# Gathering the first experts' rows, norm and top-k projection: three stages or one

## What is computed

```
h = attn0(x); h = concat(cls, h)
h = h + attn1(layernorm(h))                  # causal, rotary
h = h + moe(layernorm(h))                    # 8 gated experts, top 2
h = h + topk_attn(layernorm(h), Wq, Wk, Wv)  # 16 heads, 32 largest scores kept
h = h + selu_experts(layernorm(h))            # gate picks 2 of its logits
```

## Time and profile before

| | us |
|---|---|
| median of 3 runs (lowest, highest) | 2140.19 (2139.48, 2140.79) |
| profiled execution, its own time | 2137.56 |
| its span | 2135.8 |
| PE busy in the span | 1445.6 (68%) |
| DVE busy | 1470.7 (69%) |
| ACT busy | 825.2 (39%) |
| POOL busy | 583.4 (27%) |

### The profile page before, as it was taken

How to read it: one execution, slowest core, us unless ns; L and a number is a source line. 1 busy time by engine, 2 the same in 40 slices (tenths; PEclk the granted TensorE clock), 3 DMA queues, 4 the chain that set the end, 5 groups by cost and what they waited for, 6 DMA issues and landing times. The chain is left out here.

```text
span 2135.8 us, 35245 instructions
## 1 busy us (share of the span) xinstructions
PE 1445.6 (68%) x10364; PEld 861.4 (40%) x10397; DVE 1470.7 (69%) x4775; ACT 825.2 (39%) x2043; POOL 583.4 (27%) x1036
## 2 busy tenths in 40 slices
PE   6488887958888614999809266766676666667651
PEld 3122224524444412666505144544454445445540
DVE  3578885657777620111135499989998999899955
ACT  2266664215555301222203244444444544454430
POOL 4100001210000032000063245444554455445530
PEclk9699998969999856999958657666766677666765
DMA  5572220352330511111134600110021002100001
GB/s 161 170 258 78 75 71 8 113 153 70 79 78 21 244 45 55 45 44 44 44 102 142 172 7 1 48 33 2 1 50 31 2 1 55 26 2 1 2 1 40
DMA packets 87485, 137.61 MB, mean 64 GB/s; under 512 B 9720, under 2 KB 68000, under 8 KB 85540
## 3 DMA queue, kind: packets, MB, share of 16 engines
q1 hardware_dynamic: 84068, 127.38, 20.2%
q0 software_dynamic: 3264, 8.41, 1.2%
HBM read 82.50 MB, written 53.76 MB: 64 GB/s over the span
## 5 line engine op out<-in xcount | busy, mean ns | idle before, releaser
L1420 DVE MATCH_REPLACE8 top_left<-top_next,top_left 128x65 f32<-128x65 f32 (+15 forms) x768 | 321.9, 427 | 0.0
L1415 DVE MAX8 top_next<-top_left 128x8 f32<-128x65 f32 (+15 forms) x768 | 300.5, 431 | 0.0
L1346 POOL TENSOR_TENSOR top_e<-top_e,top_left 128x129 f32<-128x129 f32 (+15 forms) x256 | 191.2, 769 | 209.0 <-DVE top_left L1420 209.0
L1212 ACT ACTIVATE top_e<-top_ps_s,top_neg_max 128x129 f32<-128x129 f32 (+15 forms) x256 | 125.3, 489 | 284.7 <-POOL top_neg_max L1331 271.0
L686 DVE TENSOR_REDUCE tok_rowmax<-tok_ps_s 128x1 f32<-128x512 f32 x256 | 166.9, 688 | 42.8 <-PE tok_ps_s L528 40.2
L1097 PE MATMUL top_ps_pt<-ident,top_e 128*128 128x128 f32 x640 | 145.6, 354 | 70.0 <-issue 40.9
L1973 DVE TENSOR_TENSOR moe_hid<-moe_act_gate,moe_ps_h 128x512 f32<-128x512 f32 x39 | 26.8, 687 | 220.3 <-ACT moe_act_gate L1934 220.3
L686 DVE TENSOR_REDUCE rot_rowmax<-rot_ps_s 128x1 f32<-128x128 f32 (+3 forms) x256 | 115.6, 487 | 46.5 <-PE rot_ps_s L531 42.5
L659 ACT ACTIVATE tok_et<-tok_ps_st 128x1024 f32<-128x1024 f32 x128 | 124.2, 1021 | 51.0 <-PE tok_ps_st L562 51.0
L1873 PE MATMUL moe_ps_h<-moe_w,moe_rows_t 128*128 x312 | 142.7, 601 | 0.4 <-issue 0.4
L1097 PEld LDWEIGHTS top_ps_pt<-ident,top_e 128*128 128x128 f32 x640 | 101.4, 182 | 92.6 <-issue 87.6
(11 more groups left out here) (343 smaller groups left out, 3151.6 us busy)
## 6 DMA issues: line engine op xcount, KB each, us to landing
moe_w<-in_moe_w SPq DMA_DIRECT2D x3, 4096.0 KB, 24.3
moe_xs<-zeros SPq DMA_DIRECT2D x1, 5120.0 KB, 20.8
last_xs<-zeros SPq DMA_DIRECT2D x1, 5120.0 KB, 33.8
moe_rows<-moe_xs SPq DMA_DIRECT2D x40, 128.0 KB
moe_ys<-moe_y SPq DMA_DIRECT2D x38, 128.0 KB, 1.7
v_rows<-tok_va SPq DMA_DIRECT2D x4, 1024.0 KB, 5.1
tok_vs<-v_rows SPq DMA_DIRECT2D x16, 256.0 KB
v_rows<-rot_va SPq DMA_DIRECT2D x4, 1024.0 KB, 5.0
```

Source lines behind the costliest of these rows:

```text
L1212: act.activation(e[:, U % KEPT, 0:keys(U)], row(U), ACT.Exp, bias=neg_max[:, U % 4:U % 4 + 1]).then_inc(e_ok, 1)
L1346: pool.tensor_tensor(e[:, U % KEPT, 0:w], e[:, U % KEPT, 0:w], left[:, U % 4, 0:w], ALU.subtract).then_inc(prob_ok, 1)
L1415: dve.max(next8[:, U % 2, step // 2, :], left[:, U % 4, 0:keys(U)]).then_inc(pick, 1)
L1420: ins = dve.match_replace(left[:, U % 4, 0:w], next8[:, U % 2, step // 2 - 1, :], left[:, U % 4, 0:w], 0.0)
```

## The change

The first `gather_experts`, `norm` and the top `project` are replaced by one function and one stage, `gather_project`. `gather_experts` keeps only its use at the end of the program, and `project` only its use for the two earlier attentions; what they do there is as before. The order of the work in the new stage is written out by hand for each engine, without a loop:

- The class tile comes first (`tile(0)` is tile 16), then the 16 others. Each tile has a semaphore of its own for its two gathers.
- DVE does the adds, moments, reciprocal and normalisation of one tile between the steps of the quarters, five tiles ahead: quarter n stands with tile index n + 5.
- ACT takes the square root tile by tile. PE turns tile n + 5 behind quarter n.
- POOL issues all 34 gathers and only then does the third parts, of quarters 4 to 15. Those of quarters 0 to 3 are done by DVE.
- DVE clears V's padding. The normalised tiles are written to `c.ctx`, a buffer that is free at the time.
- SP issues the same weight loads at the start of this stage, so beside the gathers, and V's class row behind image 0.

The buffers of `full`, `rest`, `parts` and the PSUM halves keep their number. The diff, cut to its core:

```diff
-def norm(c, tag, fetch, ahead):
+def gather_project(c, tag, came, w, qkb, vb, weight, fetch, ahead):
...
+        xn = c.ctx
...
+        got_in = [c.sem(st, f"{came}_got_in{i}") for i in range(COUNT)]
...
+        def tile(i):
+            return i - 1 if i else NT
+        def lo_done(eng, n):
+            if n < 4:
+                eng.wait_ge(lo_first, n + 1)
+            else:
+                eng.wait_ge(lo_ok, n - 3)
         @block.sync
         def _(sp):
             c.fetch(sp, fetch)
             for dst, src in ahead:
                 sp.dma_start(dst, src).then_inc(c.upper_in, 16)
+            for b in range(B):
+                for k in range(4):
...
+                    sp.wait_ge(hi_ok, 4 * b + k + 1)
+                    sp.wait_ge(mid_ok, 4 * b + k + 1)
+                    lo_done(sp, 4 * b + k)
+                    for i in range(2):
+                        sp.dma_start(dst[b, 2 * gg + i].rearrange("i d h t -> (d h) i t"),
+                                     parts[i * HD * HG:(i + 1) * HD * HG, :, k, span(k)]).then_inc(stored[k], 16)
+                sp.wait_ge(v_ok, NQ * (b + 1))
...
+        @block.gpsimd
+        def _(pool):
+            used = pool.value_load(c.used[0:1, 0:1], min_val=0, max_val=TILES)
+            pool.memset(got[:, :, NT, :], 0.0).then_inc(clear, 1)
+            pool.wait_ge(clear, 1)
+            with pool.If(used > 0):
+                for i in range(COUNT):
+                    n = tile(i)
+                    for k in range(2):
+                        pool.indirect_dma_start(
...
+            for n in range(4, QUARTERS):
+                k = n % 4
+                pool.wait_ge(mid_ok, n + 1)
+                pool.tensor_tensor(lo[:, k, span(k)], rest[:, k % 2, span(k)], mid[:, k, span(k)], ALU.subtract
+                                   ).then_inc(lo_ok, 1)
...
+            def quarter(n):
+                b, k = n // 4, n % 4
+                which, gg = k // 2, k % 2
+                if k == 0:
+                    pe.wait_ge(t_out, NQ * (b + 1) + 1)
+                if n >= 2:
+                    pe.wait_ge(full_ok, n - 1)
...
+            turn(0)
+            turn(1)
+            class_tokens()
+            for i in range(2, NQ + 1):
+                turn(i)
+            for n in range(QUARTERS):
+                quarter(n)
+                if n + NQ + 1 < COUNT:
+                    turn(n + NQ + 1)
...
+            def first_part(n):
+                k = n % 4
+                act.wait_ge(full_ok, n + 1)
+                if n >= 4:
+                    act.wait_ge(stored[k], 16 * 2 * (n // 4))
...
+            deviation(0)
+            for i in range(1, NQ + 1):
+                deviation(i)
+                turned(i - 1)
+            turned(NQ)
+            for n in range(QUARTERS):
+                if n + NQ + 1 < COUNT:
+                    deviation(n + NQ + 1)
+                first_part(n)
+                if n:
+                    second_part(n - 1)
+                if n + NQ + 1 < COUNT:
+                    turned(n + NQ + 1)
+            second_part(QUARTERS - 1)
...
+            def add(i):
+                n = tile(i)
+                if i == 0:
+                    dve.wait_ge(clear, 1)
+                dve.wait_ge(got_in[i], 16 * 2)
+                for k in range(2):
+                    if k:
+                        dve.wait_ge(added, 2 * i + 1)
+                    dve.scalar_tensor_tensor(out=c.h[:, n, :], in0=got[:, k, n, :], scalar=weight[:, k, n:n + 1],
+                                             in1=c.h[:, n, :], op0=ALU.mult, op1=ALU.add).then_inc(added, 1)
+                dve.wait_ge(added, 2 * i + 2)
+                dve.bn_stats(stats[:, n, :], c.h[:, n, :]).then_inc(stat_ok, 1)
...
+            add(0)
+            for i in range(1, NQ + 1):
+                add(i)
+                normalise(i - 1)
+            class_tokens()
+            normalise(NQ)
+            for n in range(QUARTERS):
+                if n + NQ + 1 < COUNT:
+                    add(n + NQ + 1)
+                quarter(n)
+                if n + NQ + 1 < COUNT:
+                    normalise(n + NQ + 1)
+                if 2 <= n <= 5:
+                    third_part(n - 2)
+                if n:
+                    split(n - 1)
+            split(QUARTERS - 1)
...
-        gather_experts(c, "moe", weight, all_have=True)
...
-            norm(c, "mixed", get_top, ahead)
-            project(c, "top", *w_top, cls=True)
+            gather_project(c, "top", "moe", *w_top, weight, get_top, ahead)
```

More of the change, by code:

```diff
@@ L195, in project @@
     turns = 2 if rope else 0
-    by_position = cls and not rope
     with c.stage() as st:
@@ L2439, in _ @@
                 sp.dma_start(dst, src).then_inc(c.upper_in, 16)
[L2441 to L2455, removed]
+            for b in range(B):
+                for k in range(4):
+                    which, gg = k // 2, k % 2
+                    dst = (c.qd, c.kd[S + 1])[which]
+                    sp.wait_ge(hi_ok, 4 * b + k + 1)
[5 more added lines that the diff above has]
+                sp.wait_ge(v_ok, NQ * (b + 1))
+                for g in range(G):
+                    sp.dma_start(c.vp[b, g, 1:, :].rearrange("(n p) w -> p n w", p=P),
+                                 va[:, b, g, :, :, :].rearrange("p n h s -> p n (h s)")).then_inc(v_out, 16)
+                if b == 0:
+                    sp.wait_ge(vc_ok, 3)
+                    sp.dma_start(c.vp[:, :, 0, :], vc[:, :, :].rearrange("b (g h) s -> b g (h s)", g=G)
+                                 ).then_inc(v_out, 16)
@@ new lines, in _ @@
+            sp.wait_ge(v_out, 16 * (G * B + 1))
+            for i in range(4):
+                sp.wait_ge(stored[i], 16 * 2 * B)
+        @block.gpsimd
[8 more added lines that the diff above has]
+                        pool.indirect_dma_start(
+                            out=got[:, k, n, :], out_offset=None, in_=c.ys[came][:, :],
+                            in_offset=bass.IndirectOffsetOnAxis(ap=c.row[:, k, n:n + 1], axis=0),
+                            bounds_check=TILES * P - 1, oob_is_err=False).then_inc(got_in[i], 16)
+            with pool.Else():
+                for i in range(COUNT):
+                    pool.sem_inc(got_in[i], 16 * 2)
+            for n in range(4, QUARTERS):
[3 more added lines that the diff above has]
+                                   ).then_inc(lo_ok, 1)
@@ L2466, in _, with class_tokens @@
                                       c.ident[0:r, 0:r])
                 mm.then_inc(t_mm, 1)
+            def class_tokens():
+                pe.wait_ge(c.fetched, fetched)
+                pe.wait_ge(t_out, 1)
+                for gg in range(DC):
+                    for ch in range(DC):
+                        pe.matmul(ps_c[:, 0, gg * B:gg * B + B], w[:, ch, D + gg * P:D + gg * P + P],
+                                  c.xt[:, ch, :, 0], start=ch == 0, stop=ch == DC - 1)
+                for ch in range(DC):
+                    mm = pe.matmul(ps_c[0:B, 1, 0:D], c.xt[:, ch, :, 0], w[:, ch, 2 * D:3 * D],
+                                   start=ch == 0, stop=ch == DC - 1)
+                mm.then_inc(cls_mm, 1)
@@ L2474, in _, with deviation @@
[L2474 to L2478, removed]
+            def deviation(i):
+                n = tile(i)
+                if i == 0:
+                    act.wait_ge(eps_ok, 1)
+                act.wait_ge(aggr_ok, i + 1)
+                act.activation(rstd[:, n:n + 1], mv[:, n, 1:2], ACT.Sqrt, bias=eps[:, 0:1]).then_inc(std_ok, 1)
@@ L2481, in _, with second_part @@
                     act.activation(c.xt[:, :, :, 0], src[:, :, 0:B], ACT.Copy).then_inc(t_out, 1)
+            def first_part(n):
[3 more added lines that the diff above has]
+                    act.wait_ge(stored[k], 16 * 2 * (n // 4))
+                act.activation(hi[:, k, span(k)], full[:, k % 2, span(k)], ACT.Copy).then_inc(hi_ok, 1)
+            def second_part(n):
+                k = n % 4
+                act.wait_ge(rest_ok, n + 1)
+                act.activation(mid[:, k, span(k)], rest[:, k % 2, span(k)], ACT.Copy).then_inc(mid_ok, 1)
```

182 lines of the change are left out of this document (135 added, 47 removed).

## The result

The changed kernel takes 2112.3 us (median of 4 runs, 2111.0 to 2115.0), the kernel before beside it 2139.8 (4 runs, 2136.0 to 2140.8): a ratio of 0.988 [0.987, 0.989], so 27.5 us less. In a second series it was 2110.4 (4 runs) against 2138.5, ratio 0.987 [0.985, 0.989]. The forecast was 2108, with a range from 2099 to 2124.

What follows compares the result with a forecast made beforehand. No engine bounds all three stages (gather, norm, projection); each has its own, with barriers between. 1087.3 + 46.6 + 2.4 + 4.5 + 3.6 + 10.3 = 1154.7, plus 10.4 is 1165.1, saving 32.4: 2108, range 2099 to 2124.

Steps and rivals of the forecast that it cites:

- twelve mixed rounds: Iterations each holding a projection quarter and one tile's norm: 46.6 + 2.4 third parts + 4.5 boundaries + 3.6 clock.
- DVE becomes the bound: In the twelve mixed iterations DVE's tile work, 2.09, plus quarter work, 1.79, sets a 3.88 us round, above PE's 3.5.
- The start: Quarter 0 starts at 1087.3: the fifth tile ready at 1081.9 plus 5.4 us, bounds -2 to +4.
- costed at nothing: Weight loads issued under the gather from 1065 add no time; 3 to 4 us if they delayed the first tiles.
- 5.4 us allowance: Between the fifth tile being ready and quarter 0: its adds, moments, normalisations, class-token operations, transposes and copy, estimated at 5.4.
- The boundaries: At iterations 4, 8, 12 PE waits for ACT's copy of the turned tile: 3 x 1.5 = 4.5 us.
- The clock: PE starts the quarters at half clock: two iterations at 1.8 us extra, 3.6, then full clock taken as held.
- The tail: From PE's end to the attention's start: last part, K and V stores, landing and barrier, 10.4 us instead of 15.3.
- Stores that are not backed up: Condition of the 10.4 us after PE's end: stores of images 1 to 3, starting at 1113, end 5 us inside.
- Starved gather: DVE's instructions hold up GpSimd's gathers: 2121 at chance 0.08, or at worst 2151, slower than before, at chance 0.03.
- Clock at half throughout: PE stays at half clock through the twelve mixed iterations, saving only 13 us: 2127, chance 0.07.
- Better overlap: Clock up at once and image boundaries hidden in DVE's queue, 8 us less: 2100, chance 0.06.

Runs made afterwards that it cites:

- the copy first: The changed kernel with ACT copying the next turned tile out of PSUM before the second part of the quarter before: 2105.8 us, ratio 0.985 to the kernel before.
- the second profile: The changed kernel run and profiled again with nothing changed, as the level for the series: 2110.4 us.

## Why the prediction was right, and where its terms were off

The attention's first load was forecast at 1165.1 and came at 1170.5, 5.4 us later; the saving in the profiled execution is 27.0 of the 32.4. Term by term:

| step | forecast | measured |
|---|---|---|
| quarter 0 starts | 1087.3 | 1090.5 |
| twelve mixed rounds | 46.6 + 2.4 + 4.5 + 3.6 = 57.1 | 56.2 |
| last four quarters to PE's end | 10.3 | 10.6 |
| tail | 10.4 | 13.2 |

3.2 - 0.9 + 0.3 + 2.8 = 5.4.

- **"DVE becomes the bound", 3.88 a round**: right, and 0.08 over the mean of 3.80 (3.89 with the class column, 3.71 without). 49.0 for twelve of them with the third parts stands against 49.2 with the copy first; part of that match is luck, since by the measured rounds DVE's work is 12 x 3.80 + 2.4 = 48.0 and 1.2 is left of the boundaries. The stage that already did this tile by tile gave the price with its gaps.
- **The start** is the first step that failed. The weights' loads were "costed at nothing", with "3 to 4" if they delayed the first tiles. They did: 6.01 us of idle DVE, and with the loads moved back quarter 0 stood at 21.7 us into the stage, 3.1 earlier, and near the forecast (1087.3 - 1065 = 22.3). The cover that I named, 15 us of gather, hides the loads from PE but not from the gathers, whose rows come through the same DMA engines (0.98 busy, 402 GB/s while DVE waited for the first rows). Of the 3.2 some 0.7 is not this: the first gather began at 1067.77 and not at 1067.1. The 5.4 us allowance behind the fifth tile was right: 1085.18 to 1090.50 is 5.3. Little or nothing of the 3.1 could be had back by moving the loads, though, as the two runs with late loads show.
- **The boundaries**: place and cause right (ACT's copy behind the second part), 3.6 us against 4.5. **The clock**: 3.5 against 3.6 in this profile, but not where I put it: one quarter at half clock at the start and not two, and it was not held behind the waits at quarters 4 and 8. "I take it as held" was wrong in kind, and the sum right by two errors, which is luck: in the second profile the clock cost 1.1. With boundary waits of 0.5 us it was 1.00 at every boundary (three kernels).
- **The tail** is the second step that failed, by 2.8: the last part 4.0 us for 3.3, K's second half 1.85 for 1.4, V 3.5 for 3.0, and landing 3.8 for 2.7. The landing was misread: before, it was 1197.51 - 1193.93 = 3.6 from the end of V's issues too, the class row's issue lay within it, and the 2.7 was counted from that one's end; now it is 1170.49 - 1166.69 = 3.8. The last part is late in DVE's queue: V and `rest` of quarter 14 and V of quarter 15 stand ahead of `rest` of quarter 15 (1157.35 to 1158.62), which the sum left out. "Stores that are not backed up" held for SP's queue, whose last pair was issued 0.5 us after its part (1161.78, part done at 1161.30). It did not hold for the DMA engines, at 0.88 from 1160 to 1167: what a second queue issues beside SP waits there, as the run with V on ACT's queue shows. How much of the 3.8 is this, no run shows.
- **The rivals.** Starved gather, 2121 and 2151: refuted in the changed kernel (1.354 apart) and alone (1.453 apart under back-to-back instructions). The Trainium skill, page SBUF — State Buffer, section "SBUF: two separate sides", has an exclusive lock between a VectorE instruction with two SBUF inputs and a GpSimd one that reads SBUF. The trace agrees in kind only: of an indirect DMA's issue the runs show 0.26 us held up at most under instructions of 0.49 us back to back, and 0.50 once in the changed kernel; GpSimd's arithmetic wasn't tried. Clock at half throughout, 2127: refuted, 0.90 in the mixed window. Better overlap, 2100: the copy-first kernel has nearly all of it (boundary waits of 0.47, full clock from quarter 0 on in its profile) and stands at 2105.8, the rest being start and tail (3.2 + 2.8).

## What to carry to other kernels

Where one queue works serially for tens of microseconds and the others wait at a barrier, fuse the stages tile by tile; the price of the mixed round is the sum of the bound engine's instructions with their semaphore gaps, and an existing tile-by-tile stage gave it here to 0.08 of 3.80 us. A fused order without that overlap is worth nothing here (7 us slower). Inside the fused loop, put the short hand-over that another engine waits for ahead of bulk work in the same queue: here two instructions in ACT's order were worth 4.6 us. And look at the DMA engines' share before loads are laid under a gather or stores onto a second queue: here the loads (0.98 busy) held the first rows up by 5 us of DVE's time, and the stores (0.88 to 0.97) went no faster from two queues. Moving the loads or the stores alone lowered the median by nothing.

## What the runs showed of the hardware that I had not expected

- Indirect DMAs of GpSimd beside a DVE that works back to back: 1.00 us becomes 1.00 to 1.07 or 1.25 to 1.26 under two-input instructions of 0.49 us, and 1.08 under float32 copies of 0.43 us (one run each).
- The granted clock after PE's waits of 1.4 to 2.1 us inside a stretch that is otherwise 75% busy: quarter 8 came at half clock in the first profile and at full in the second, behind the same 1.43 us. Behind the boundary waits of 0.5 us (three kernels), and with filler matmuls in front (one profile), it was full each time.
- DVE and ACT began up to 9.4 us after the PE work that they waited for while POOL issued gathers, in the kernel where GpSimd does all third parts (15 to 17 us in all). Its cause is open.
